# A three-layer graph network with a routed feed-forward block on one core: search rows, step sums, the surplus matmul and the rows' copies change their places

## The chip, the cores and the metric

One Trainium2 chip; the kernel runs on one of its cores. The metric is the device time of one execution in microseconds (us), the median of several runs.

## The reference

6250 nodes with 256 features, 200000 edges sorted by their target.

```python
def _layernorm(x): return (x - mean(x)) / sqrt(var(x) + 1e-5)

src, dst = edges + one loop per node
dinv = rsqrt(segment_sum(1, dst))
def conv(h, W, b): return segment_sum((h @ W)[src] * dinv[src] * dinv[dst], dst) + b

h = layernorm(x)
h = relu(conv(h, W1, b1)); h = relu(conv(h, W2, b2)); x = x + conv(h, W3, b3)

n = layernorm(x)
weights = n @ wr + br                 # one per node
sel = the (6250 // 2 - 1) nodes of highest weight
y = (gelu(n[sel] @ w1 + b1) @ w2 + b2) * weights[sel]
out = x + n + scatter(y, sel)
```

## The kernel before, in words

Nodes are taken in 49 tiles of 128. Each layer multiplies a matrix of edge counts (target by source) with scaled rows of features. For most target tiles (32, 32 and 34 in the three layers) that matrix is built densely as fp16 from one-hots and multiplied tile by tile; a (target tile, source tile) product of 128x128 by 128x512 is a *unit*, run by `unit` (L1403). For the remaining sparse tiles Pool gathers single rows by indirect DMA (`fetch_row`, L2021), and a step with a one-hot sums them (L1412). 5749 units stand in one written-out order `UNIT`; everything else is hung on unit numbers: `SUM_AT`, `SPILL_AT`, `OVER_AT`, `TURN_AT`, `ROWS_TURN_AT` and so on. Each engine runs its instructions strictly in its own written order. TensorE follows `units(limit)`, DVE and ACT follow `upto(limit)` over the same numbers, SP walks them at the end of its queue.

**Front.** The edges must be found first: the kernel counts, for 10 columns of windows, how many edges lie below each window. DVE and ACT count over a coarse list, Pool fetches one search row for each window (L1926), and DVE's `lows` counts in those rows (L846) and makes `step_cols` ("low of step zero", L851). TensorE's `chunk_steps` (the step sums, L1581, 56 instructions) spreads them to the steps, DVE's `place_steps` (L857 to L859) turns them into edge addresses, first for 6 chunks and then for 13, and Pool's `fetch_edges` (L1932) brings the edges. Beside this, the first product of each of the 49 tiles (x times the centred W1) is made by `product_first` (L1361) and copied out by ACT (`out_first`, L1722). Of those, `BEFORE` stand ahead of the step sums, `BESIDE` right behind them, two for each step j in the loop over the batches of edges, and `LATE` near its end. ACT and DVE also measure x's variance: `measure_x(n)` (L866 to L871) takes the seven tiles of one group, and its end lets SP fetch another group (`fetch_x`, L2084). TensorE's 190 ns loads at L1602 belong to a small product in the same stretch. In the batch loop DVE unpacks edges, TensorE transposes them and ACT copies them out.

**Building and layer one.** From unit 98 on, dense tiles are built from pairs of steps (`step`, L1375: one-hots from DVE, evacuated by ACT, L1756) while units of layer one run in between, at the pace of `DUE`.

**Surplus.** A window can hold more edges than its quota; the rest goes through a loop of at least one round (`spill`, in Pool, TensorE and ACT). Pool fetches a list entry, edges, the old sums and, once SP has stored the layer's rows (`rows_out`), the rows themselves (L1995), and makes a one-hot (L1997 to L2001). TensorE multiplies (L1444) when its unit counter reaches `SPILL_AT[l]`, ACT copies (L1797), Pool adds and stores (L2008 to L2011) and raises `overflowed`. SP then fetches the stored sums for each target tile (L2158, from unit `OVER_AT`), ACT scales them (L1766), and DVE's `sum_tile` (L1050, L1052) adds them to the tile's PSUM bank. The unit that starts a tile in a bank waits for the sum of the bank's previous tile.

**Choice and feed-forward.** When the early tiles of layer three are done, a first list of nodes is chosen and their rows are gathered. The first block has four groups of 128 rows. `turn` (L1484) transposes a group on TensorE into one PSUM bank at units 5721, 5727, 5733 and 5739, and waits for DVE's copy of the group before it; `settle` (L1206) is that copy. DVE reaches all four copies at unit 5743, behind the norms (L1103 to L1120) of the tiles summed just before. The hidden layer (L1497) begins behind the last unit.

Of the kernel before, what the change touches and what calls it, by code (L numbers as in the profile page):

```python
# [20 lines left out]
TILES = -(-N // P)  # L21
# [154 lines left out]
GROUPS = TILES // KC  # L176
# [47 lines left out]
UNITS = len(UNIT)  # L224
START = [min(u for u, (p, i) in enumerate(UNIT) if p == q) for q in range(len(Q))]
END = [max(u for u, (p, i) in enumerate(UNIT) if p == q) + 1 for q in range(len(Q))]
SPILL_AT = [2 * TILES + 32, START[TILES] + 85, START[2 * TILES] + 85]
OVER_AT = [SPILL_AT[0] + 2, SPILL_AT[1] + 50, SPILL_AT[2] + 50]


def sum_units():
# [27 lines left out]
BLOCKS = blocks_of()  # L259
# [5 lines left out]
TIES_AT = COUNT_AT[-1] + COUNT_SPACE  # L265
LISTING_AT = TIES_AT + 55
ROWS_TURN_AT = [UNITS - 28 + 6 * s for s in range(len(BLOCKS[0]))]
ROWS_SETTLE_AT = UNITS - 6
NORM_AT = [SUM_AT[2 * TILES + NORM_FROM[g + 1] - 1] if g != EARLY_GROUPS else
           max(SUM_AT[2 * TILES + NORM_FROM[g + 1] - 1], LISTING_AT + 3) for g in range(len(NORMS))]  # L270
TURN_AT = [u + 12 for u in SUM_AT]
# [52 lines left out]


DUE = due_units()
BEFORE, BESIDE, LATE = 10, 3, 6
DVE_COLS = 4
ACT_GROUPS, DVE_GROUPS = (0, 2, 4, 6), (1, 3, 5)
STAGE = (0, 1, 2, 1, 0, 1, 2)  # L330
# [185 lines left out]
def graph(nc, ctx, space, gathered_in, ones, route, small, smalli, b1_sb, br_b, x, x_turned, dst_rows, dst_over, dst_last, edges, gw, gb, wr, br, w1, b1, w2, b2, pair_dram, out):  # L516
# [269 lines left out]
    with nc.Block() as block:  # L786
        @block.vector
        def _(dve):
# [6 lines left out]
            def done(ins, name=None):  # L795
                noted(ins, name)
                dve.wait_ge(c_dve, steps["all"])
# [63 lines left out]
            def measure_x(n):  # L861
                g = DVE_GROUPS[n]
                s, tiles = slice(g * KC, g * KC + KC), staged[STAGE[g]]
                dve.wait_ge(x_in[STAGE[g]], 16 * (STAGE_TURN[g] + 1))
                for i in range(KC):
                    noted(dve.bn_stats(stats[:, i, :], tiles[:, i]))  # L866
                dve.wait_ge(c_dve, steps["all"])
                for i in range(KC):
                    noted(dve.bn_aggr(aggr[:, 0, i, :], stats[:, i, :]))
                dve.wait_ge(c_dve, steps["all"])  # L870
                dve.tensor_copy(spread_of[:, s], aggr[:, 0, 0:KC, 1]).then_inc(measured, 1)  # L871
# [8 lines left out]
            dve.wait_ge(p_order, 1)  # L880
            done(dve.tensor_copy(ordered[:, 1:2], disorder))
            done(dve.tensor_scalar(ordered[:, 0:1], ordered[:, 1:2], 0.0, None, ALU.is_equal))
            measure_x(0)
            lows()
            dve.wait_ge(c_pool, CONSTANTS + LATER_CONSTANTS)
            noted(dve.tensor_copy(iota_two[:], iota16[:].unsqueeze(2).broadcast_to([P, WC, 2])))
            done(dve.tensor_copy(iota_many[:], iota16[:, 0:P].unsqueeze(2).broadcast_to([P, P, 4])))
            place_steps(0)
            place_steps(1)

# [350 lines left out]
            def upto(limit):  # L1241
                for u in range(at["u"] + 1, limit + 1):
# [18 lines left out]
                        spread(0)  # L1261
                    if u == LISTING_AT + 1:
                        take_list(0)
                    if u == ROWS_SETTLE_AT:
                        for s in BLOCKS[0]:
                            settle(s)
                    for q in LOWS.get(u, ()):
                        low_tile(q)
                    if u == MEASURE_AT:
# [623 lines left out]
        def _(pool):  # L1893
# [55 lines left out]
            def each(ins):  # L1949
                ins.then_inc(more_step, 1)  # L1950
                pool.reg_add(m, m, 1)
                pool.wait_ge(more_step, pool.snap(m))
                pool.sem_inc(passed, 1)
# [10 lines left out]
            def spill(l):  # L1964
# [10 lines left out]
                with pool.Fori(0, again):  # L1975
                    each(pool.memset(which, 0.0))
                    with pool.Fori(0, inner):
# [12 lines left out]
                        pool.indirect_dma_start(more_old[:, 0:width], None, target,  # L1990
                                                bass.IndirectOffsetOnAxis(target_i, 0)).then_inc(old_in, 16)
                        landed(more_in)
                        if l >= 0:
                            pool.wait_ge(rows_out[l], 16 * (TILES if l else GROUPS))
                            pool.indirect_dma_start(more_rows, None, row_dram[l],  # L1995
                                                    bass.IndirectOffsetOnAxis(pair_i[:, 1:2], 0)).then_inc(more_rows_in, 16)
                        each(pool.tensor_copy(node, pair_i[:, 0:1]))  # L1997
                        each(pool.tensor_tensor(node, node, item[:, 1:2], ALU.subtract))
                        each(pool.tensor_scalar(bad, node, wide, 16384.0, ALU.is_ge, ALU.mult))
                        each(pool.tensor_tensor(node, node, bad, ALU.add))  # L2000
                        each(pool.tensor_scalar(more_hot, iota16[:, 0:P], node, None, ALU.is_equal))  # L2001
                        if l >= 0:
                            landed(more_rows_in)
                        pool.sem_inc(more_ready, 1)
# [244 lines left out]
```

## Time and profile before

| | before |
|---|---|
| median of 3 runs | 1876.97 us (1875.36 to 1879.09) |
| profiled execution | 1876.37 us |
| its span, first to last instruction | 1874.6 us |
| TensorE (PE) busy | 1808.8 us, 96% |
| VectorE (DVE) busy | 1072.4 us, 57% |
| ScalarE (ACT) busy | 509.8 us, 27% |
| GpSimd (POOL) busy | 1107.0 us, 59% |
| mean granted clock of TensorE | 0.982 |

A line of the timeline gives start and length in us, engine, source line, operation, output<-input, how many instructions are merged, and in brackets how long the engine was idle before and what released it. PEld is TensorE's loading of weights, which overlaps its matmuls. The granted clock is 1.00 at 2.4 GHz and 0.50 at 1.2 GHz. A matmul's end is modelled, so neighbours overlap in the listing.

### The profile page before, as it was taken

How to read it: one execution, taken by the hardware profiler on the slowest of the kernel's cores; microseconds unless marked ns; L12 is line 12 of the kernel's file. 1: busy time of each engine (PE TensorE's matmuls, PEld its weight loads, DVE VectorE, ACT ScalarE, POOL GpSimd, SP SyncE). 2: the span in 40 equal slices, each digit the busy share in tenths (PEclk: the TensorE clock that was granted, in tenths of full speed). 3: DMA queues.
4: the chain of work that ended last, by engine and by line, in shares of the span. 5: the costliest groups of instructions: out<-in, count | busy, mean ns of one | idle time of the engine just before them, and what ended most of it. 6: DMA issues, size and time to landing. Idle time of an engine off the chain costs nothing.

```text
span 1874.6 us, 28149 instructions
## 1 busy us (share of the span) xinstructions
PE 1808.8 (96%) x10093; PEld 1060.7 (57%) x10093; DVE 1072.4 (57%) x2904; ACT 509.8 (27%) x1043; POOL 1107.0 (59%) x1198
## 2 busy tenths in 40 slices
PE   7998999999999999999999999999999999989898
PEld 6765666666665555555555555544444444447655
DVE  6898999888876666432222222216455656866422
ACT  6755423444444445121111111110000000012020
POOL 6423666665656664277777777727777777731401
PEclk8979999999999999999999999999999999999999
DMA  9626566576655665677777777757987888660200
GB/s 322 217 85 246 181 211 214 203 250 232 214 199 177 206 212 179 242 243 240 248 245 241 236 235 235 231 183 274 330 312 271 313 283 303 226 211 36 87 15 21
DMA packets 170640, 403.36 MB, mean 215 GB/s; under 512 B 29612, under 2 KB 122722, under 8 KB 157833
## 3 DMA queue, kind: packets, MB, share of 16 engines
q1 hardware_dynamic: 119856, 263.42, 39.4%
q0 software_dynamic: 50592, 138.13, 23.3%
q8 instruction: 84, 1.38, 0.3%
q14 instruction: 52, 0.42, 0.1%
q10 hardware_dynamic: 56, 0.03, 0.0%
HBM read 282.57 MB, written 118.89 MB: 214 GB/s over the span
## 4 chain that ended last, share of the span: by engine, by line
PE 83%; DVE 8%; DMA 5%; ACT 2%; issue 1%; POOL 1%; POOLq 0%; DVEq 0%; ACTq 0%
PE ag L1403 28%; PE pw L1403 22%; PE ag L1412 10%; PE pw L1375 7%; PE pw L1497 3%; DMA space_rows<-extra,space_rows 3%; PE both L1429 2%; PE pw L1429 2%; PE ag L1510 2%; PE pw L1510 2%; PE ag L1497 1%; PE both L1421 1%; ACT space_ring L1756 1%; DMA space_rows<-deg_dram,space_rows 1%; DVE space_tables L1011 1%
## 5 line engine op out<-in xcount | busy, mean ns | idle before, releaser
L2021 POOL DMA_INDIRECT space_rows<-row_dram,src_s x947 | 965.8, 1020 | 396.1 <-issue 201.1
L1403 PE MATMUL ag<-space_a,space_ring 128*128 128x512 f16 x2107 | 621.6, 379 | 6.3 <-DVE space_work L1052 5.8
L1412 PE MATMUL ag<-space_rows,hots 128*128 128x512 f16 x947 | 359.1, 379 | 5.8 <-DVE space_b L1052 5.8
L1375 PE MATMUL pw<-space_tables 128*128 128x147 f16 (+1 forms) x2022 | 323.0, 243 | 13.5 <-ACT space_ring L1756 10.1
L1375 PEld LDWEIGHTS pw<-space_tables 128*128 128x128 f16 x2022 | 226.6, 114 | 189.5 <-ACT space_ring L1756 22.0
L1756 ACT ACTIVATE space_ring<-pw 128x784 f16<-128x784 f32 (+1 forms) x257 | 219.1, 857 | 231.6 <-PE pw L1375 224.6
L1011 DVE TENSOR_TENSOR space_tables<-iota_two,space_tables 128x588 f16<-128x588 f16 (+1 forms) x506 | 256.2, 506 | 0.0
L1403 PEld LDWEIGHTS ag<-space_a,space_ring 128*128 128x128 f16 x2107 | 197.0, 97 | 98.3 <-DVE space_work L1052 6.0
L1007 DVE TENSOR_TENSOR space_tables<-iota_many,space_tables 128x512 f16<-128x512 f16 x506 | 211.8, 419 | 17.9 <-PE pw L1375 16.6
L1403 PE MATMUL pw<-space_b,space_ring 128*128 128x512 f16 x735 | 189.3, 379 | 0.0
L1403 PE MATMUL pw<-space_a,space_ring 128*128 128x512 f16 x686 | 168.6, 381 | 0.0
L1766 ACT ACTIVATE space_work<-space_work,per_node 128x256 f32<-128x256 f32 x147 | 73.7, 503 | 334.0 <-DMA space_work<-extra 334.0
L1412 PEld LDWEIGHTS ag<-space_rows,hots 128*128 128x128 f16 x947 | 107.2, 113 | 81.2 <-DVE space_b L1052 7.5
L1057 DVE SCALAR_TENSOR_TENSOR space_a<-pw,per_node,space_a 128x256 f16<-128x256 f32 x49 | 23.7, 484 | 207.3 <-ACT space_a L1780 207.3
L1774 ACT ACTIVATE space_work<-both,gb_sb 128x128 f32<-128x128 f32 x196 | 61.2, 364 | 247.3 <-PE both L1421 247.3
L1403 PEld LDWEIGHTS pw<-space_b,space_ring 128*128 128x128 f16 x735 | 71.9, 98 | 78.5
L1403 PE MATMUL ag<-space_b,space_ring 128*128 128x512 f16 x441 | 115.1, 379 | 0.0
L1403 PEld LDWEIGHTS pw<-space_a,space_ring 128*128 128x128 f16 x686 | 67.5, 99 | 79.0 <-issue 1.9
L1064 DVE TENSOR_TENSOR hots<-iota_many,key_s 128x512 f16<-128x512 f16 x238 | 106.5, 460 | 1.2
L1050 DVE SCALAR_TENSOR_TENSOR space_work<-ag,per_node,space_work 128x256 f32<-128x256 f32 x78 | 37.6, 482 | 80.8 <-PE ag L1403 56.1
L1403 PE MATMUL pw<-space_a,space_tables 128*128 128x512 f16 x294 | 78.0, 389 | 0.0
L1050 DVE SCALAR_TENSOR_TENSOR space_b<-pw,per_node,space_work 128x256 f32<-128x256 f32 x20 | 9.7, 483 | 111.0 <-PE pw L1403 77.8
(424 smaller groups left out, 1925.5 us busy)
## 6 DMA issues: line engine op xcount, KB each, us to landing
space_ring<-adj SPq DMA_DIRECT2D x48, 1568.0 KB, 7.4
adj<-space_ring SPq DMA_DIRECT2D x34, 1568.0 KB, 6.1
space_tables<-adj SPq DMA_DIRECT2D x17, 1568.0 KB, 7.3
space_work<-extra SPq DMA_DIRECT2D x147, 128.0 KB
space_rows<-row_dram,src_s POOLq DMA_INDIRECT x947, 4.0
extra<-space_tables SPq DMA_DIRECT2D x14, 896.0 KB
space_b<-in_x_turned SPq DMA_DIRECT2D x7, 896.0 KB, 14.9
space_a<-in_x SPq DMA_DIRECT2D x7, 896.0 KB, 9.4
```

The lines of the kernel that those rows point to most:

```text
L1007: dve.tensor_tensor(olo[:, r], iota_many[:], slo[:, 2 * j:2 * j + 4].unsqueeze(1).broadcast_to([P, P, 4]), ALU.is_equal)
L1011: dve.tensor_tensor(ohi[:, r, :, 0:n], iota_two[:, 0:n].unsqueeze(1).broadcast_to([P, 2, n, 2]), keys.unsqueeze(2).broadcast_to([P, 2, n, ...
L1064: dve.tensor_tensor(hots_area[:, n % (HOTS // 4)], iota_many[:], key_s[:, s:s + 4].unsqueeze(1).broadcast_to([P, P, 4]), ALU.is_equal).the ...
L1375: pe.matmul(pw[v % 2][:, half, at_c:at_c + n], olo[:, j % RING // 2, :, j % 2 * 2 + i], ohi[:, j % RING // 2, j % 2, 0:n, i], start=s == F ...
L1403: mm = pe.matmul(bank(q), a[:, k, :], hh[l][:, k, :], start=i == 0, stop=i == TILES - 1)
L1412: pe.matmul(bank(q), hots_area[:, hot_at, :, g - SPOT_GROUPS[SPOT_GROUP_OF[g]][0]], slots[g % GR], start=i == 1, stop=i == n).then_inc(g_u ...
L1429: mm = pe.matmul(ph[l - 1], fresh[:, q % 2, f, :], gw_sb[:, l, f, :], start=f == 0, stop=f == HALVES - 1)
L1497: mm = pe.matmul(bank_of(hidden_banks[h % 3])[:, 0:n], w1_sb[:, k, m * P:(m + 1) * P], xt[c][:, k, 0:n], start=k == 0, stop=k == HALVES - 1)
L1510: mm = pe.matmul(bank_of(out_banks[s % 2])[0:n, 0:D], hid[c % 2][:, m, i * P:i * P + n], w2_sb[:, m, :], start=m == 0, stop=m == HM - 1)
L1756: act.activation(target[:, :, d:d + n].rearrange("p s (h d) -> p s h d", h=2), pw[v % 2][:, :, 0:n // 2 * TILES].rearrange("p h (d s) -> p ...
L1766: act.activation(ep[:, q % 2], ep[:, q % 2], ACT.Copy, scale=unfactor[:, l, t:t + 1]).then_inc(e_scaled, 1)
L2021: pool.indirect_dma_start(slots[g % GR], None, row_dram[STEP_LAYER[g]], bass.IndirectOffsetOnAxis(src_s[:, s:s + 1], 0)).then_inc(g_in[g % ...
```

## The change

Five edits. (1) The surplus matmul of layer one goes from unit 130 to unit 116; the unit from which sums are fetched, 132, stays. (2) `BEFORE` is 12 in place of 10, so two first products go ahead of the step sums, and the loop beside the batches has two fewer (it ends one step sooner). (3) DVE's first `measure_x` stands behind `lows` and two copies of iotas, ahead of `place_steps`. (4) Each of the first block's four copies stands one unit behind its turn (5722, 5728, 5734, 5740). (5) In Pool's `spill`, the rows' fetch with its wait stands behind the five small instructions that make the one-hot.

```diff
-SPILL_AT = [2 * TILES + 32, START[TILES] + 85, START[2 * TILES] + 85]
-OVER_AT = [SPILL_AT[0] + 2, SPILL_AT[1] + 50, SPILL_AT[2] + 50]
+SPILL_AT = [2 * TILES + 18, START[TILES] + 85, START[2 * TILES] + 85]
+OVER_AT = [SPILL_AT[0] + 16, SPILL_AT[1] + 50, SPILL_AT[2] + 50]
...
-ROWS_SETTLE_AT = UNITS - 6
+ROWS_SETTLE_AT = {u + 1: s for s, u in enumerate(ROWS_TURN_AT)}
...
-BEFORE, BESIDE, LATE = 10, 3, 6
+BEFORE, BESIDE, LATE = 12, 3, 6
...
             done(dve.tensor_scalar(ordered[:, 0:1], ordered[:, 1:2], 0.0, None, ALU.is_equal))
-            measure_x(0)
             lows()
             dve.wait_ge(c_pool, CONSTANTS + LATER_CONSTANTS)
             noted(dve.tensor_copy(iota_two[:], iota16[:].unsqueeze(2).broadcast_to([P, WC, 2])))
             done(dve.tensor_copy(iota_many[:], iota16[:, 0:P].unsqueeze(2).broadcast_to([P, P, 4])))
+            measure_x(0)
             place_steps(0)
             place_steps(1)
...
-                    if u == ROWS_SETTLE_AT:
-                        for s in BLOCKS[0]:
-                            settle(s)
+                    if u in ROWS_SETTLE_AT:
+                        settle(ROWS_SETTLE_AT[u])
...
                         landed(more_in)
-                        if l >= 0:
-                            pool.wait_ge(rows_out[l], 16 * (TILES if l else GROUPS))
-                            pool.indirect_dma_start(more_rows, None, row_dram[l],
-                                                    bass.IndirectOffsetOnAxis(pair_i[:, 1:2], 0)).then_inc(more_rows_in, 16)
                         each(pool.tensor_copy(node, pair_i[:, 0:1]))
                         each(pool.tensor_tensor(node, node, item[:, 1:2], ALU.subtract))
                         each(pool.tensor_scalar(bad, node, wide, 16384.0, ALU.is_ge, ALU.mult))
                         each(pool.tensor_tensor(node, node, bad, ALU.add))
                         each(pool.tensor_scalar(more_hot, iota16[:, 0:P], node, None, ALU.is_equal))
+                        if l >= 0:
+                            pool.wait_ge(rows_out[l], 16 * (TILES if l else GROUPS))
+                            pool.indirect_dma_start(more_rows, None, row_dram[l],
+                                                    bass.IndirectOffsetOnAxis(pair_i[:, 1:2], 0)).then_inc(more_rows_in, 16)
                         if l >= 0:
                             landed(more_rows_in)
```

## Rows read from the trace of the kernel before

**Rows 1.** The page: the chain that ended last, by engine.
```profile
PE 83%; DVE 8%; DMA 5%; ACT 2%; issue 1%; POOL 1%; POOLq 0%; DVEq 0%; ACTq 0%
```

**Rows 2.** TensorE's waits, whole span: us in total, times, longest.
```profile
PE pw L1484 <- DVE space_b L1206: 10.1, 3, 6.2
...
PE ag L1403 <- DVE space_work L1052: 5.8, 1, 5.8
PE ag L1581 <- DVE step_cols L851: 4.8, 1, 4.8
```

**Rows 3.** Timeline of the front, 23 to 48 us.
```profile
23.40 1.38 POOL L1926 DMA_INDIRECT space_rows<-in_dst_rows,tile_i  x1 [0.30 <-DVE space_ring L838]
...
28.36 2.39 DVE L866 BATCH_NORM_STATS2 stats<-space_a 128x6 f32<-128x256 f32 x7
...
29.16 1.03 PE L1361 MATMUL ag<-gw_sb,space_b 128*128 128x256 f32 x4
...
31.47 0.34 DVE L846 TENSOR_SCALAR_CACHE_REDUCE space_rows<-space_rows,cols 128x128 f32<-128x128 f32 x1
...
34.95 12.11 PE L1581 MATMUL ag<-step_cols,space_ring 128*128 128x3 f32 x56 [4.77 <-DVE step_cols L851]
...
36.02 0.99 SPq L2084 DMA_DIRECT2D space_a<-in_x  x2
...
47.17 0.17 DVE L857 TENSOR_TENSOR step_f<-ag,step_at 128x13 f32<-128x13 f32 x1 [8.09 <-PE ag L1581]
```

**Rows 4.** DMA issues at 23.3 to 23.6 us: count, us to landing.
```profile
space_rows<-in_dst_rows,tile_i POOLq DMA_INDIRECT x1, 6.8
```

**Rows 5.** Stretches: us, PE, PEld, DVE, ACT, POOL busy, PEclk, DMA share, GB/s.
```profile
33.00:34.00 1.00, 0.00 (x0) 0.00 (x0) 1.00 (x9) 0.97 (x5) 0.00 (x0) 0.94 1.08 312
...
35.00:47.00 12.00, 12.00 (x57) 12.00 (x57) 1.04 (x5) 5.23 (x22) 5.76 (x6) 0.50 0.79 226
...
173.00:174.00 1.00, 0.00 (x0) 0.00 (x0) 0.00 (x0) 0.00 (x0) 0.10 (x1) 0.91 0.00 0
...
177.00:180.00 3.00, 2.81 (x11) 1.47 (x12) 2.45 (x8) 0.00 (x0) 2.39 (x3) 0.50 0.97 363
...
1665.00:1666.00 1.00, 0.00 (x0) 0.00 (x0) 0.96 (x5) 0.00 (x0) 0.00 (x0) 0.73 0.82 269
```

**Rows 6.** Weight loads of two lines: ns min/median/max, first and last start.
```profile
L1581 PEld LDWEIGHTS ag<-step_cols,space_ring x56: 286/333/333, 35.0 to 46.6; 128*128 128x128 f32 x56
...
L1602 PEld LDWEIGHTS ag<-cols,space_rows x2: 190/191/192, 51.7 to 51.8; 128*128 128x128 f32 x2
```

**Rows 7.** Timeline, the last two products beside the batches.
```profile
89.24 1.03 PE L1361 MATMUL ag<-gw_sb,space_b 128*128 128x256 f32 x4
...
90.10 1.03 PE L1361 MATMUL both<-gw_sb,space_b 128*128 128x256 f32 x4
```

**Rows 8.** Timeline of Pool: the surplus rows of layer one.
```profile
154.45 0.94 POOL L1995 DMA_INDIRECT space_rows<-row_dram,space_rows  x1 [34.41 <-DMA row_dram<-space_a]
...
157.77 1.13 POOL L2001 TENSOR_SCALAR space_rows<-iota,space_rows 128x128 f16<-128x128 f16 x1 [0.21 <-POOL space_rows L2000]
```

**Rows 9.** Timeline of TensorE around the surplus matmul of layer one.
```profile
160.57 0.59 PE L1403 MATMUL ag<-space_a,space_ring 128*128 128x512 f16 x2
...
165.18 0.38 PE L1444 MATMUL both<-space_rows 128*128 128x512 f16 x1
...
177.19 1.03 PE L1403 MATMUL ag<-space_a,space_ring 128*128 128x512 f16 x2 [5.79 <-DVE space_work L1052]
```

**Rows 10.** Timeline around the first block's turns and copies.
```profile
1661.76 0.17 DVE L1103 TENSOR_SCALAR rstd_x<-aggr 128x3 f32<-128x3 f32 x1
...
1665.88 0.42 DVE L1206 COPY space_b<-pw 128x256 f32<-128x256 f32 x1
...
1666.44 0.66 PE L1484 MATMUL pw<-ident,space_b 128*128 128x128 f32 x2 [6.22 <-DVE space_b L1206]
...
1672.59 2.32 PE L1403 MATMUL pw<-space_a,space_tables 128*128 128x512 f16 x10
```

## The prediction, made before the changed kernel was run

> **What bounds the kernel now.** I read the page's chain first, then TensorE's waits, then the timeline around the places the diff touches. TensorE holds 83% of the chain that ended last [rows 1]. So what counts is where it stands still or runs at half its clock, and any such time that goes away before its long middle is carried to the end: the list of TensorE's waits has nothing longer than 1 us behind which Pool's row fetches or a DMA stand. Of its five longest entries three lie where the diff works [rows 2]: 4.8 us for the step sums (L1581) behind DVE's `step_cols`, 5.8 us in layer one behind DVE's first tile sum (L1052), and 10.1 us in three waits of the rows' turns (L1484) behind DVE's copies (L1206), 6.2 of it in one. 0.2% of this kernel, about 3.8 us, is what a measurement can tell from no change.
>
> **Search rows and two products (front).** Before, DVE measures seven tiles of x from 28.36 us and only then counts the search rows from 31.47, so 3.1 us stand ahead of the count; TensorE's tenth product starts at 29.16 and ends at 30.19, the step sums start at 34.95 [rows 3]. Nothing in the rows needs that order. The last search row is issued at 23.40 and takes 6.8 us to land, 30.2 [rows 3, 4]; the ten counts start at 28.4 and want the last row 9 steps of 0.27 later, about 30.8, which leaves 0.6 us. So `step_cols` is ready at about 31.8. TensorE now has two more products in its gap; at 0.86 us from start to start, as at 89.24 and 90.10 [rows 7], they end at 29.16 + 1.72 + 1.03 = 31.9. The sums start at 31.9, **3.0 us** sooner. The measuring itself lands in DVE's wait for the sums, which was 8.09 us long before its end at 47.17 [rows 3]: from about 32.5 (behind the two iota copies) to 35.7. It signals SP's fetch of x group 3, which SP's own queue let go only at 36.02 [rows 3], so that costs nothing; without that cover it would cost up to the 3.2 us of the measuring. ACT's two extra copies go between its squares, and it is idle later; nothing.
>
> **The clock of the step sums.** TensorE has no work between 30.19 and 34.95; in it the granted clock falls (0.94 in 33 to 34) and the sums run at 0.50, the 1.2 GHz level, all of 35 to 47 [rows 3, 5]. With the products up to 31.9 the sums begin at 2.4 GHz. A sum is a weight load with three columns behind it, and the load took 333 ns at half clock where the same form took 190 ns at full (L1602) [rows 6]; the second of the two L1602 loads started 0.11 us behind the first, against 12.11/56 = 0.216 a sum at half clock [rows 3]. So I take two sums for one as long as the full level lasts. How long it lasts no row shows for such work: after TensorE fell idle the level was lost some 3.7 us later here (0.94 is 0.12 us at half), 2.4 us later at 171.4, 5.2 us later at 1660.2 [rows 5, 9, 10]. I take 3.7, the nearest, which saves as much: **3.7 us**, from 0 to 6 (all 56 at full clock).
>
> A load of the weights does not get faster with the clock by the Trainium skill, "TensorE: Matmul & The Clock Gate", section "LDWEIGHTS (loading the stationary operand)": it prices a load by its columns at a fixed rate, with no warm and cold form beside it. By that the 3.7 would be 0 and the change worth that much less. The trace disagrees: 190 against 333 ns.
>
> The two products are missing later in the loop beside the batches: the pair at 89.24 and 90.10 goes [rows 7], 1.7 us of TensorE in a stretch where DVE's unpacking and TensorE's transposes wait for each other in turn, and no row shows which of them would be last without it. I take something under half: **0.7 us**, 0 to 1.7. From 47 to 131 us the front is DVE's and TensorE's own work in turn, so all of this moves the start of layer one. Pool's edge fetches (19 at 1.25 us) start at 36.2 in place of 39.3 and feed batches well ahead.
>
> **Surplus matmul 14 units sooner.** In layer one TensorE passes the matmul (L1444) at 165.18 without waiting for it; from there Pool's add and store, SP's fetch, ACT's scaling and DVE's two sums run in one chain until TensorE goes on at 177.19, 12.0 us later, after 5.79 us of standing still [rows 9]. In units and pairs the 116th unit ends ahead of 160.57 [rows 9]; put there, the chain ends at 172.6, TensorE arrives at 171.4 as before, and 1.2 us of stall are left: **4.6 us**. ACT's spill copy keeps its place right behind an evacuation. What must be there by 160.6: Pool fetched the surplus rows at 154.45, when layer one's rows were stored, and its one-hot was done at 158.90 [rows 8]; the new order of Pool's copies takes the one-hot into the wait of 34.41 us, so that only the landing is left. That part I cost at nothing, since TensorE's margin, 6.3 us before, is still 1.6. In layers two and three the same order only fills Pool's waits; TensorE does not wait there. The stall also cost the clock: it fell in 173 to 174, and 177 to 180 ran at 0.50 [rows 5], so 3 us of work went at half speed. A stall of 1.2 should not lose it: **1.5 us** more, 0 to 2. Next late is that 1.2.
>
> **Rows' copies behind their turns.** TensorE's second turn waits 6.22 us for DVE's first copy, which stands behind three tiles' norms: DVE takes `rstd_x` at 1661.76 and copies at 1665.88 [rows 10]. In the new order the first copy follows that instruction at once: 1661.93 to 1662.35, and with the 0.14 between the old copy's end and TensorE's start, the turn goes at 1662.5 in place of 1666.44. The copies take 0.42 each between norms of about 1.2; the turns then come every 1.55 us or so (six units at 0.216 and a turn), which DVE meets within 0.3 us. Six, six and ten units and three turns later the last unit ends at about 1668.4; before, it ended at 1672.59 + 2.32 = 1674.9 [rows 10], with 1665 to 1666 already at 0.73 of the clock [rows 5]. **6.5 us**, down to 4.7 if the 2.3 us that are left still cost the clock. The norms' end moves from 1665.9 to 1667.3, ahead of the next tile sum. Everything behind it (chosen rows, hidden layer) hangs on the last unit or on this sum.
>
> **Sum.** 3.0 + 3.7 + 0.7 + 4.6 + 1.5 + 6.5 = 20.0 us. The profiled execution took 1876.37 us around its span of 1874.6; that is 0.6 below the median of the runs, 1876.97. So 1856.4 for a profiled one and 1857 for the median. By the bounds: least 2.5 (the last search row half a us late) + 0 + 0 + 3.2 (1.4 lost to ACT in the new chain) + 0 + 4.7 = 10.4, most 3.1 + 6 + 1.7 + 4.7 + 2 + 6.6 = 24.1.
>
> **Rivals.**
> Rival one: the sums run no faster (a load bound by something other than the clock, or the level falls at once). For it: f32 loads were never seen in a long row at full clock. Against: 190 and 333 ns [rows 6]. It takes 3.7 off: 1860.7. The skill's rule above is this rival.
> Rival two: the shortened stalls still lose the clock. For it: the stall at 171.4 lost it after 2.4 us, and 2.3 us are left at the turns. It takes 1.5 + 1.8 off: 1860.3.
> Rival three, slower: the surplus matmul itself becomes the wait. It stands in TensorE's order, so from 160.6 on each us by which Pool's rows are late is a us of TensorE, with the pairs and evacuations behind it. It outweighs the rest only from 20 us of lateness on, a landing behind 180 us. For it: the Pool fetch sits behind 34 us of row stores. Against: the one-hot, already behind that wait, was done at 158.9 [rows 8].
> Rival four: the parts move and the end does not, because something beside TensorE paces the middle (Pool's 947 row fetches). Against: none of TensorE's listed waits [rows 2] is for them. Under 3.8 us gained.
>
> **How the numbers follow.** Forecast 0.70 (its own range 1854 to 1860), rival one 0.12, rival two 0.12, rival four 0.04, rival three 0.02. Rivals one and two are faster too, so faster is 0.94. The range takes in the forecast and both of them together (1864) and reaches 1865 for a late chain at the surplus; low, 1853, is every bound at its best.
>
> **What would show it.** Right: L1581 starting at about 32 with no wait before it, and a clock of 1.00 in its first microseconds; DVE's second `step_f` at about 40 to 41; L1444 some 4.6 us nearer to layer one's first unit, and the wait of L1403 behind L1052 near 1 us; the first L1206 ahead of the last norms, and the turns' wait near 2.3 us. Wrong: L1444 with a wait for Pool, a new wait of L846 for a DMA, or the later layers longer by what the front gave.

## The result, and the profile after

The changed kernel takes 1859.37 us (median of 6 executions, 1858.35 to 1862.86) against 1877.24 us before (median of 6): a ratio of 0.9908, interval 0.9898 to 0.9919. By the medians that is 17.9 us, 0.95%, faster; 20.0 us were forecast, and 1859.4 lies in the range of 1853 to 1865. The profiled execution took 1858.35 us around a span of 1856.6, 18.0 us less than before. Behind line 1264 a line of the kernel after has a number one lower than before (L1403 is L1402, L1444 is L1443, L1484 is L1483, L1581 is L1580); only among the moved lines, in DVE's front and in Pool's `spill`, is the offset another.

From the page after, busy time by engine, and the chain by engine:

```profile
PE 1801.6 (97%) x10093; PEld 1056.3 (57%) x10093; DVE 1071.9 (58%) x2904; ACT 510.1 (27%) x1043; POOL 1098.4 (59%) x1198
...
PE 80%; DVE 8%; DMA 7%; ACT 2%; issue 1%; POOL 1%; POOLq 0%; DVEq 0%; ACTq 0%
```

TensorE does the same 10093 matmuls in 7 us less busy time, and its page has 11 us less idle time around them; it is still the chain. TensorE's waits after, whole span (us in total, times, longest), against [rows 2]:

```profile
PE pw L1483 <- DVE space_b L1206: 6.1, 3, 2.8
...
PE ag L1402 <- DVE space_work L1052: 1.4, 1, 1.4
```

The wait of the step sums is gone from the list, that for the first tile sum fell from 5.8 to 1.4, and the longest of the rows' turns from 6.2 to 2.8 us (one of the second block now; the first block's is 2.28). The front after, against [rows 3]:

```profile
28.38 0.35 DVE L846 TENSOR_SCALAR_CACHE_REDUCE space_rows<-space_rows,cols 128x128 f32<-128x128 f32 x1
...
31.64 0.17 DVE L851 SCALAR_TENSOR_TENSOR step_cols<-cols 128x10 f32<-128x10 f32 x1
...
32.01 9.52 PE L1580 MATMUL ag<-step_cols,space_ring 128*128 128x3 f32 x56
...
35.70 0.15 DVE L857 TENSOR_TENSOR step_f<-ag,step_at 128x6 f32<-128x6 f32 x1
...
41.63 0.17 DVE L857 TENSOR_TENSOR step_f<-ag,step_at 128x13 f32<-128x13 f32 x1 [5.51 <-PE ag L1580]
```

The counts of the search rows start 3.1 us sooner and wait for no row; the sums start behind the twelfth product with no wait, and take 9.52 us in place of 12.11. The granted clock (the column ahead of DMA share and GB/s) in stretches of the kernel after, against [rows 5]:

```profile
34.00:35.00 1.00, 1.00 (x10) 1.00 (x9) 0.97 (x3) 0.97 (x5) 0.00 (x0) 0.83 1.21 294
35.00:44.00 9.00, 9.00 (x37) 8.55 (x38) 3.04 (x22) 6.63 (x29) 5.84 (x7) 0.50 0.87 236
...
166.00:170.00 4.00, 3.29 (x27) 2.24 (x28) 3.96 (x12) 0.00 (x0) 3.09 (x4) 1.00 0.95 375
...
1648.00:1650.00 2.00, 0.00 (x0) 0.00 (x0) 1.83 (x7) 0.43 (x2) 0.00 (x0) 1.00 0.80 266
1650.00:1656.00 6.00, 5.86 (x29) 3.08 (x30) 4.51 (x17) 0.17 (x1) 0.00 (x0) 1.00 0.66 219
```

The sums run at 2.4 GHz until 34.66 (0.83 is two thirds of a microsecond at full) and then at 1.2. TensorE's record has no gap there, so the clock fell while the sums ran, and not behind a wait. Behind the shortened stall of the surplus (TensorE goes on at 166.71), and in and behind the turns' wait, the clock stays full. Surplus and turns after, against [rows 8 to 10]:

```profile
115.45 0.64 POOL L1996 TENSOR_SCALAR space_rows<-iota,space_rows 128x128 f16<-128x128 f16 x1 [0.21 <-POOL space_rows L1995]
...
148.27 1.07 POOL L1999 DMA_INDIRECT space_rows<-row_dram,space_rows  x1 [32.18 <-DMA row_dram<-space_a]
...
154.27 0.38 PE L1443 MATMUL both<-space_rows 128*128 128x512 f16 x1
...
166.71 0.60 PE L1402 MATMUL ag<-space_a,space_ring 128*128 128x512 f16 x2 [1.43 <-DVE space_work L1052]
...
1649.37 0.17 DVE L1103 TENSOR_SCALAR rstd_x<-aggr 128x3 f32<-128x3 f32 x1
...
1649.57 0.42 DVE L1206 COPY space_b<-pw 128x256 f32<-128x256 f32 x1
...
1650.14 0.41 PE L1483 MATMUL pw<-ident,space_b 128*128 128x128 f32 x2 [2.28 <-DVE space_b L1206]
...
1653.57 2.32 PE L1402 MATMUL pw<-space_a,space_tables 128*128 128x512 f16 x10
```

The one-hot starts 33 us ahead of the rows' fetch, the matmul does not wait, the stall is 1.43 us, and the first copy follows `rstd_x` at once. Where the 18.0 us came from, by the start of the same instruction in both traces:

| place | before | after | gained so far |
|---|---|---|---|
| second `step_f` | 47.17 | 41.63 | 5.54 |
| first unit of layer one | 131.09 | 124.88 | 6.21 |
| TensorE goes on behind the first tile sum | 177.19 | 166.71 | 10.48 |
| transposes of that tile's result (L1421) | 182.31 | 170.18 | 12.13 |
| first gathered step (L1412) | 200.05 | 189.13 | 10.92 |
| surplus matmul of layer three | 1248.48 | 1237.96 | 10.52 |
| first turn | 1658.55 | 1646.18 | 12.37 |
| hidden layer | 1674.74 | 1655.73 | 19.01 |
| end of the span | 1874.6 | 1856.6 | 18.0 |

Three steps have no edit near them: 1.2 us lost between 182 and 200, 1.9 won between 1248 and 1658, 1.0 lost behind the hidden layer's start.

### The profile page after: what moved, and what is told of

It reads as the page before. It is cut to its first block, busy times and chain, and to the rows that moved or that the text cites. A ratio compares the mean times of both kernels' runs of the same rounds, so it can differ in the third digit from the quotient of the medians.

```text
span 1856.6 us, 28149 instructions
## 1 busy us (share of the span) xinstructions
PE 1801.6 (97%) x10093; PEld 1056.3 (57%) x10093; DVE 1071.9 (58%) x2904; ACT 510.1 (27%) x1043; POOL 1098.4 (59%) x1198
## 4 chain that ended last, share of the span: by engine, by line
PE 80%; DVE 8%; DMA 7%; ACT 2%; issue 1%; POOL 1%; POOLq 0%; DVEq 0%; ACTq 0%
PE ag L1402 28%; PE pw L1402 21%; PE ag L1411 10%; PE pw L1374 7%; PE pw L1496 3%; DMA space_rows<-extra,space_rows 2%; PE pw L1428 2%; PE both L1428 2%; PE ag L1509 2%; PE pw L1509 2%; PE ag L1496 1%; PE both L1420 1%; ACT space_ring L1755 1%; DMA space_work<-extra 1%; DVE space_tables L1011 1%
## 5 line engine op out<-in xcount | busy, mean ns | idle before, releaser
L1402 PE MATMUL ag<-space_a,space_ring 128*128 128x512 f16 x2107 | 620.3, 378 | 1.9 <-DVE space_work L1052 1.4
L1402 PEld LDWEIGHTS ag<-space_a,space_ring 128*128 128x128 f16 x2107 | 196.7, 97 | 94.0 <-DVE space_work L1052 1.6
L1402 PE MATMUL pw<-space_b,space_ring 128*128 128x512 f16 x735 | 189.3, 379 | 0.0
L1402 PE MATMUL pw<-space_a,space_ring 128*128 128x512 f16 x686 | 167.2, 379 | 0.0
L1402 PEld LDWEIGHTS pw<-space_b,space_ring 128*128 128x128 f16 x735 | 71.8, 98 | 78.5
L1402 PE MATMUL ag<-space_b,space_ring 128*128 128x512 f16 x441 | 115.1, 379 | 0.0
L1402 PEld LDWEIGHTS pw<-space_a,space_ring 128*128 128x128 f16 x686 | 67.3, 99 | 77.8
L1402 PE MATMUL pw<-space_a,space_tables 128*128 128x512 f16 x294 | 75.5, 379 | 0.0
```

The costliest lines, as they stand in the source:

```text
L1402: mm = pe.matmul(bank(q), a[:, k, :], hh[l][:, k, :], start=i == 0, stop=i == TILES - 1)
```

## Experiments

Each is the changed kernel with the edit shown, timed in 4 to 6 executions beside the kernel before (medians there 1876.94 to 1877.23).

**Copies back at one unit.**

```diff
-ROWS_SETTLE_AT = {u + 1: s for s, u in enumerate(ROWS_TURN_AT)}
+ROWS_SETTLE_AT = UNITS - 6
```

> The changed kernel with one edit undone: the four copies of the rows stand at one unit again, behind the norms. Theory (the parts add): the second turn waits 6.2 us again, TensorE falls to 1.2 GHz in it, and the 6.6 us that lay between the first turn and the hidden layer come back: 1859.4 + 6.6 = 1866.0 us. Rival (the hidden layer would have waited for something else, the chosen rows or the list): under 2 us come back, 1859.4 to 1861.4 us.

1865.54 us (ratio 0.9939, 0.9926 to 0.9952), 6.2 more than the changed kernel: the theory holds. TensorE at the second turn and at the hidden layer:

```profile
1656.88 0.66 PE L1484 MATMUL pw<-ident,space_b 128*128 128x128 f32 x2 [6.21 <-DVE space_b L1206]
...
1665.14 1.88 PE L1497 MATMUL ag<-space_b,space_ring 128*128 128x512 f32 x4
```

From the first turn (1649.00) to the hidden layer it is 16.14 us, as before (16.19), against 9.55 in the changed kernel. In the trace the edit is worth its 6.6 us, and the medians, 6.2 apart, agree: nothing behind it takes much of them.

**Surplus matmul back at unit 130.**

```diff
-SPILL_AT = [2 * TILES + 18, START[TILES] + 85, START[2 * TILES] + 85]
-OVER_AT = [SPILL_AT[0] + 16, SPILL_AT[1] + 50, SPILL_AT[2] + 50]
+SPILL_AT = [2 * TILES + 32, START[TILES] + 85, START[2 * TILES] + 85]
+OVER_AT = [SPILL_AT[0] + 2, SPILL_AT[1] + 50, SPILL_AT[2] + 50]
```

> The changed kernel with the surplus matmul back at unit 130. Theory one (the stall alone counts, as its clock was taken back by the fetch of the next tile's stored sums): the wait for the first tile sum is 5.8 us instead of 1.4, and the time is 1859.4 + 4.4 = 1863.8 us. Theory two (the clock counts too, as predicted): 1859.4 + 4.4 + 1.6 = 1865.4 us. They differ in where the first gathered step of layer one starts against that of the changed kernel (189.1 us): 193.5 by theory one, 195.1 by theory two.

1865.41 us (0.9940, 0.9927 to 0.9952), 6.0 more; first gathered step at 195.34. Theory two holds: the clock counts. TensorE goes on at 171.41 after 5.71 us, and the stretches around it are at half clock:

```profile
168.00:171.00 3.00, 0.00 (x0) 0.00 (x0) 0.61 (x2) 1.01 (x2) 2.06 (x3) 0.51 0.84 309
171.00:174.00 3.00, 2.59 (x11) 1.48 (x12) 2.53 (x7) 0.00 (x0) 2.39 (x3) 0.50 0.96 369
```

The 1.2 us that the changed kernel gave back between 182 and 200 have another source than the place of the surplus matmul. In the changed kernel the third tile's stored sums, issued by SP at 173.09, were scaled by ACT at 182.06, 9.0 us later; before it was 185.01 and 192.97, 8.0 us. Here it is 9.0 again (179.23 and 188.27). All twelve traces with twelve products ahead of the sums have 8.6 to 9.2, and the only other one with ten has 7.8. So every kernel with twelve paid it; two traces with ten do not show that the products are the cause, and it stays open.

**x measured first again.**

```diff
+            measure_x(0)
             lows()
...
-            measure_x(0)
             place_steps(0)
```

> The changed kernel with the measuring of x ahead of the search rows' counts again; twelve products still stand ahead of the step sums. Theory (the clock falls in the gap behind the last product): step_cols at about 34.9, TensorE idle 3 us from 32.0, the sums at 1.2 GHz for nearly all of their length, second step_f at 46.8 to 47.2 in place of 41.6, time 1859.4 + 5.3 = 1864.7 us. Rival (two more products carry the clock into the sums, so that only the 3.0 us of the start are lost): second step_f at 44.6, time 1862.4 us.

1865.03 us (0.9940, 0.9928 to 0.9952), 5.7 more. The theory holds, though the second `step_f`, at 46.42, is 0.4 us sooner than it says. TensorE's sums, and DVE's second addresses:

```profile
34.90 11.42 PE L1580 MATMUL ag<-step_cols,space_ring 128*128 128x3 f32 x56 [2.78 <-DVE step_cols L851]
...
46.42 0.17 DVE L857 TENSOR_TENSOR step_f<-ag,step_at 128x13 f32<-128x13 f32 x1 [8.09 <-PE ag L1580]
```

The clock fell at 35.7 (0.84 in 35 to 36), 0.8 us into the sums; two more products ahead do not carry the level over a gap of 2.8 us.

**Ten products again.**

```diff
-BEFORE, BESIDE, LATE = 12, 3, 6
+BEFORE, BESIDE, LATE = 10, 3, 6
```

> The changed kernel with ten products ahead of the step sums again. Theory (the level is lost some 3.7 us behind the last product, whatever sums run in between): the sums start at 31.9 behind an idle 1.7 us, the granted clock falls at about 33.9 instead of 34.7, second step_f at 42.3 in place of 41.6; with the two products back in the loop beside the batches, 0.7, the time is 1859.4 + 1.4 = 1860.8 us. Rival (the sums start at 1.2 GHz at once after the gap): second step_f at 44.2, 1859.4 + 2.6 + 0.7 = 1862.7 us. Second rival (products in the loop hide fully): 1859.4 + 0.7 = 1860.1 us.

1861.15 us (0.9911, 0.9897 to 0.9926), 1.8 more, with 1858.72 to 1865.24 too wide to part 1.4 from 0.7. In its trace the sums start at 31.78 behind 1.45 us of idleness, the clock falls at 34.16, and the second `step_f` is at 41.86, 0.2 later than in the changed kernel: the rival of a cold start is out. So the sums begin at full clock without the two products too, once the search rows are counted first. The profiled execution was the slowest one, 1865.24 us, and most of what it lost lies far from the edit:

```profile
156.65 3.03 POOL L2007 TENSOR_TENSOR space_rows<-space_rows 128x256 f32<-128x256 f32 x1 [5.49 <-DMA space_rows<-extra,space_rows]
```

Pool's add of the surplus took 3.03 us in place of 0.93, a later small instruction 1.93 in place of 0.23, and TensorE's stall behind the tile sum was 4.61 in place of 1.43. In layer three this execution lost 1.6 us more (see the last run).

**Pool's old order.** The rows' fetch and its wait stand ahead of the five small instructions.

```diff
+                        if l >= 0:
+                            pool.wait_ge(rows_out[l], 16 * (TILES if l else GROUPS))
+                            pool.indirect_dma_start(more_rows, None, row_dram[l],
...
                         each(pool.tensor_copy(node, pair_i[:, 0:1]))
...
-                        if l >= 0:
-                            pool.wait_ge(rows_out[l], 16 * (TILES if l else GROUPS))
-                            pool.indirect_dma_start(more_rows, None, row_dram[l],
```

> The changed kernel with Pool's old order in the surplus loop: the fetch of the rows, with its wait, stands ahead of the five small instructions again. Theory (costed at nothing): the fetch is issued at 148.3 us as in the changed kernel, the five instructions end some 4.5 us later (as from 154.45 to 158.90 before), at 152.8, the surplus matmul is reached at 154.3 and does not wait: 1859.4 us, within 0.5. Rival (the five instructions are stretched beside VectorE's one-hots, as Pool's add was in the run with ten products, 3.03 us instead of 0.93): the matmul waits, its stall and that behind it grow by 1 to 3 us, 1860.4 to 1862.4 us.

1858.68 us (0.9911, 0.9897 to 0.9925): no difference, as the theory has it. The one-hot, and with it all that the matmul needs of Pool's own work, ends at 153.07:

```profile
152.36 0.71 POOL L2000 TENSOR_SCALAR space_rows<-iota,space_rows 128x128 f16<-128x128 f16 x1 [0.21 <-POOL space_rows L1999]
```

TensorE passes the matmul at 154.44 without waiting. The edit is a margin of a microsecond, not a gain.

**Surplus at unit 112.**

```diff
-SPILL_AT = [2 * TILES + 18, START[TILES] + 85, START[2 * TILES] + 85]
-OVER_AT = [SPILL_AT[0] + 16, SPILL_AT[1] + 50, SPILL_AT[2] + 50]
+SPILL_AT = [2 * TILES + 14, START[TILES] + 85, START[2 * TILES] + 85]
+OVER_AT = [SPILL_AT[0] + 20, SPILL_AT[1] + 50, SPILL_AT[2] + 50]
```

> The changed kernel with the surplus matmul four units sooner still, unit 112. The rows landed at 152.6 us, the matmul would be reached at about 152.8. Theory: it does not wait or by some tenths, the 1.4 us that are left of the stall behind the first tile sum go, and the time is 1859.4 - 1.3 = 1858.1 us. Rival (the third tile's stored sums, fetched later by SP, set the pace): the stall goes, the next product's wait grows by as much, 1859.4 us.

1861.50 us (0.9915, 0.9901 to 0.9929): no gain, inside the spread. Neither theory holds: TensorE does not wait at the matmul, but the stall is 1.11 us, not 0. TensorE was at the matmul only at 154.48, because its clock came back at 129.5 at the start of layer one, not at 126.8; and from the matmul to the end of the stall it is 13.88 us, against 12.44 in the changed kernel's trace. Pool's small instruction behind the store took 1.98 us in place of 0.23. Pool's instruction and VectorE's next one behind a pause, in the changed kernel and then here:

```profile
161.74 0.23 POOL L2012 TENSOR_SCALAR space_rows<-space_rows 128x1 f32<-128x1 f32 x1 [1.79 <-DMA extra<-space_rows]
161.96 0.23 DVE L1018 TENSOR_TENSOR space_ring<-space_ring,ident 128x128 f16<-128x128 f16 x1 [0.30 <-ACT space_ring L1755]
```

```profile
161.61 1.98 POOL L2012 TENSOR_SCALAR space_rows<-space_rows 128x1 f32<-128x1 f32 x1 [1.78 <-DMA extra<-space_rows]
163.94 0.25 DVE L1018 TENSOR_TENSOR space_ring<-space_ring,ident 128x128 f16<-128x128 f16 x1 [0.43 <-ACT space_ring L1755]
```

In the changed kernel the instruction falls into a pause between VectorE's one-hots. Here it comes into their unbroken row and ends when the row does. The other kernel with the matmul at unit 112 (all edits, below) has the same 1.98, 13.88 and 1.12. So the four units bring the matmul forward and lengthen the chain behind it by about as much.

The front of this execution is the clearest view of the sums; its DVE, its loads (ns min/median/max), and its clock:

```profile
39.03 0.17 DVE L857 TENSOR_TENSOR step_f<-ag,step_at 128x13 f32<-128x13 f32 x1 [2.98 <-PE ag L1580]
...
42.85 0.29 DVE L916 TENSOR_TENSOR space_work<-space_ring,step_base 128x128 f32<-128x128 int32 x1 [3.05 <-DMA space_ring<-in_edges,step_i]
```

```profile
L1580 PEld LDWEIGHTS ag<-step_cols,space_ring x56: 186/192/338, 31.8 to 38.5; 128*128 128x128 f32 x56
```

```profile
32.00:37.00 5.00, 5.00 (x47) 5.00 (x46) 3.91 (x20) 4.93 (x23) 0.75 (x1) 1.00 0.93 234
37.00:38.00 1.00, 1.00 (x8) 1.00 (x8) 0.00 (x0) 0.97 (x4) 0.69 (x2) 0.65 0.56 131
```

With the same code in the front the level held until 37.3. 46 loads in 5 us are one every 0.109 us. The second `step_f` came 2.6 us sooner than in the changed kernel's trace, and all of it went into a wait of 3.05 us for the first edges: DVE's first unpacking (L916) starts at 42.85, there at 42.56.

**Row copies further ahead.**

```diff
-ROWS_SETTLE_AT = {u + 1: s for s, u in enumerate(ROWS_TURN_AT)}
+ROWS_SETTLE_AT = {UNITS - 26: 2, UNITS - 19: 3}
...
+                        if q == len(Q) - 2:
+                            settle(0)
                         sum_tile(q)
+                        if q == len(Q) - 2:
+                            settle(1)
```

> The changed kernel with the first row copy ahead of the tile sum that precedes it on VectorE, the second right behind that sum, the third and fourth ahead of the norms of the late group. Theory: the second turn's wait of 2.28 us goes (VectorE is at that sum at 1646.7 us, the first turn ends at 1646.8), the hidden layer starts up to 2.2 us sooner and the time is 1859.4 - 2.0 = 1857.4 us. Rival (VectorE is the bound there: sums and norms in one row, so the copies only move the wait to the third or fourth turn): under 0.5 us gained.

1858.34 us (0.9904, 0.9890 to 0.9918). First turn to hidden layer is 7.56 us against 9.55, so the theory's 2.0 us are there in the trace; one wait is left, at the fourth turn (L1487 is this kernel's number for L1483):

```profile
1654.25 0.41 PE L1487 MATMUL pw<-ident,space_b 128*128 128x128 f32 x2 [0.45 <-DVE space_b L1206]
```

In the median only 1.0 shows, less than these runs can tell apart.

**Three products between the sums.**

```diff
+            between = {5: BEFORE, 9: BEFORE + 1, 13: BEFORE + 2}
             for c in range(CH):
                 chunk_steps(c)
-            for t in range(BEFORE, BEFORE + BESIDE):
-                product_first(t)
+                if c in between:
+                    product_first(between[c])
```

> The changed kernel with the three products that follow the step sums put between them, behind the 6th, 10th and 14th chunk. Theory one (the granted clock falls because the sums alone do little, and a product between them holds it): clock 1.00 through 32 to 40, second step_f at 40.8 us in place of 41.6, first transposes of the batches at 43.9 in place of 45.8, time 1859.4 - 1.9 = 1857.5 us. Theory two (the level is lost a few us into the sums all the same): the products run at half clock ahead of the last sums, second step_f at 46 to 47, first transposes at about 49, time 1859.4 + 3.2 = 1862.6 us.

1865.07 us (0.9937, 0.9923 to 0.9951), 5.7 more, and neither theory holds. The clock stayed at 1.00 until 38.2, nearly as theory one has it, but the time went theory two's way for a reason in neither:

```profile
41.75 2.05 PE L1360 MATMUL both<-gw_sb,space_b 128*128 128x256 f32 x4 [2.74 <-ACT space_b L1722]
```

The third product needs a bank that ACT copies out only behind its squares; TensorE stood still, and the last 12 sums ran behind it at half clock. Second `step_f` 46.26.

**First addresses ahead of the measuring.**

```diff
-            measure_x(0)
             place_steps(0)
+            measure_x(0)
             place_steps(1)
```

> The changed kernel with the first addresses of steps ahead of the measuring of x. Theory (the run with the surplus at unit 112 had its second step_f at 39.0 us and its first unpacking waited 3.05 us for the first edges, fetched behind the first step_f at 35.6): first step_f at about 34.5, so the first edges land near 41.5; with the second step_f at 41.4 to 41.9, as in most runs, nothing is gained, 1859.4 us; if it comes at 39, the first unpacking waits about 2 us and not 3. Rival (the measuring, now up to 37.8 us, holds up SP's fetch of x, which before came at 36.5, and with it the products): 0.5 to 1.5 us lost.

1860.08 us (0.9908, 0.9895 to 0.9921): no gain, as the theory has it for a second `step_f` at 41.87. The first one came at 35.01 only, 1.95 us behind the start of the sums, and these started only at 33.06, behind products that ran later in this execution. What earlier addresses give when the second `step_f` comes at 39 was not seen.

**The same, and two products between the sums.** Behind the 6th and the 12th chunk, the third product behind the sums.

```diff
+            between = {5: BEFORE, 11: BEFORE + 1}
...
-            for t in range(BEFORE, BEFORE + BESIDE):
+                if c in between:
+                    product_first(between[c])
+            for t in range(BEFORE + 2, BEFORE + BESIDE):
                 product_first(t)
```

> As the kernel with the addresses first, and with two of the three products that follow the step sums put between them (behind the 6th and the 12th chunk); for the third ACT's copies would be late. Theory: clock 1.00 up to at least 38 us, the 56 sums and two products end at 40.2 to 40.6, second step_f at about 40.5, first unpacking at 41.5 by its edges in place of 42.6, time 1859.4 - 1.1 = 1858.3 us. Rival (the third product, at half clock behind the sums, and the transposes take it back): 1859.4 us.

1864.40 us (0.9932, 0.9920 to 0.9945), 5.0 more: theory and rival both missed. The clock fell at 36.9 (0.96 in 36 to 37) although a product had run from 34.90, and the second product stood at half clock ahead of the last 20 sums:

```profile
39.00 2.05 PE L1360 MATMUL ag<-gw_sb,space_b 128*128 128x256 f32 x4
40.84 4.27 PE L1580 MATMUL ag<-step_cols,space_ring 128*128 128x3 f32 x20
```

Second `step_f` 45.15. A product between the sums is a sure 0.9 to 1.8 us on the path against a level that it may or may not hold (until 38.2 in the run before, 36.9 here).

**All of them.** The last edit with the copies further ahead and the surplus at unit 112.

> The changed kernel with the addresses first, two products between the sums, the copies of the rows ahead of the tile sum and its norms, and the surplus matmul at unit 112. Theory (parts add): 1.1 + 1.9 + 0.3 less, 1859.4 - 3.3 = 1856.1 us; the wait for the rows' copies at most 0.5 us. Rival (what the front gives is taken back before the first unit of layer one): 1857.4 us.

1861.32 us (0.9914, 0.9901 to 0.9927): both missed, for the products between (second `step_f` 45.23, clock down at 36.5); turn to hidden layer again 7.56 us. Of the versions tried none beats the changed kernel by more than these runs can tell; the copies further ahead are the one edit with a gain of its own in the trace.

**The changed kernel again,** unaltered.

> The changed kernel itself, unaltered, for the spread between executions. Theory (the clock's falls and rises come at times that differ between executions of the same work): median 1859.4 us, second step_f between 39 and 42 us, full clock at the start of layer one between 125.7 and 129.7 us; single executions from 1858 to 1863 us. Rival (the differences of the other runs come from their edits): step_f at 41.6, clock back at 126.6, as in the first profile.

1858.60 us (0.9897, 0.9883 to 0.9911), 1856.99 to 1862.70. The theory holds, with wider spans than I gave: the second `step_f` at 40.53, the clock down at 35.8 in the sums and back only at 131.3 at the start of layer one, and the fastest execution a microsecond below the span. The profiled execution is the one of 1862.70. Stretches of its clock, and a wait in layer three:

```profile
35.00:36.00 1.00, 1.00 (x10) 1.00 (x10) 0.93 (x11) 1.00 (x7) 0.00 (x0) 0.88 1.02 146
```

```profile
PE ag L1411 <- DVE space_b L1052: 2.6, 1, 2.6
```

```profile
1532.00:1536.00 4.00, 3.92 (x19) 1.85 (x20) 3.76 (x14) 0.51 (x1) 2.64 (x3) 1.00 0.40 114
```

The same wait in the kernel before, and the stretch behind it:

```profile
PE ag L1412 <- DVE space_b L1052: 2.6, 1, 2.6
```

```profile
1539.00:1542.00 3.00, 3.00 (x9) 1.10 (x8) 2.82 (x10) 0.51 (x1) 1.99 (x2) 0.53 0.49 161
```

A wait of 2.6 us cost the clock before and did not here. From the third surplus matmul to the first turn it is 410.07 us before and 408.22 in the first trace of the changed kernel, and every other run has one of the two lengths (408.1 to 408.4, or 409.7 to 410.2), the one with the copies put back 410.2. In all six traces with the longer one the clock fell at this wait, in the eight others it held. So the 1.9 us won there come from the clock's level at one wait that no edit touches, and five of the twelve later runs lost them again. From the hidden layer to the end it is 199.86 before, 200.87 after, and others have either (199.6 to 199.9 in three, 200.7 to 201.0 in nine): the 1.0 us lost there can come with and without these edits, and what decides it stays open.

## Why the prediction held, and where it did not

**Step sums sooner, 3.0.** Right: 34.95 to 32.01 is 2.94, and no row was late. It is not so in each execution: in four traces (Pool's old order, addresses first, and the two kernels built on that) the products ended later and the sums started at 33.05 to 33.21. The prediction puts the measuring at nothing, and that is not quite so: DVE takes the first `step_f` only behind it, at 35.70 and without a wait. With the first addresses ahead it came 1.95 us behind the start of the sums, which would be 33.96 here (an estimate from that run). So the first edges are asked for some 1.7 us later than they could be, and they are the next to be late; what that costs is not shown. Undone with the clock that goes with it, the earlier count costs 5.7 us.

**Full clock in the sums, 3.7.** That the sums run faster at full clock is right, the size was off: 2.6 in this execution (5.54 less 2.94). A load of this form runs at 192 ns and every 0.109 us at full clock, over 46 of them in a row; so rival one falls, and with it, for these f32 loads, the pricing of the Trainium skill, "TensorE: Matmul & The Clock Gate", "LDWEIGHTS (loading the stationary operand)", without a clock. The step that failed is "the level was lost some 3.7 us later here ... I take 3.7, the nearest". That span was read behind an idle TensorE, and here TensorE was never idle. In the seven traces with the changed kernel's front unaltered the level fell 2.2 to 5.5 us into the sums, 2.9 in the middle one; 3.7 lies in that span, above its middle. And where it held longest it gave nothing more, since the first edges were the next to be late (the unpackings that waited for them start at 42.6 to 43.0): "feed batches well ahead" was the second step that failed. In the changed kernel's trace DVE's first unpacking already waits 0.17 us for them. It starts 5.3 us sooner than before (47.83 to 42.56), and 2.9 of that is the earlier start of the sums, so the clock's term could pass on some 2.3 us, and not 6. And the second `step_f`, at 41.63, was not at the 40 to 41 named as a sign.

**Two products, 0.7.** 6.21 less 5.54 is 0.67, but that it meets the forecast is luck: from the second `step_f` to the first unit it is 83.3 to 84.2 us in the runs with twelve products whose edges were less than 1 us late, and with ten it is 83.9 (before) and 84.6. The term is not shown. Nor is it shown that the two products carry the clock into the sums, since with ten these began at full clock too.

**Surplus, 4.6, and its clock, 1.5.** Right: the matmul is 4.7 us nearer to the first unit (34.09 to 29.39), a stall of 1.43 is left in place of the 1.2 forecast, and 4.3 us arrive where TensorE goes on (10.48 less 6.21); the clock's share was 1.65 at the tile's transposes (12.13 less 10.48). Undone, the two cost 6.0 us against the 6.1 summed. What the text lacked is the next late one, the third tile's stored sums: in all twelve traces with twelve products they took 0.9 to 1.5 us back against before, also with the matmul at its old place, and no run shows why. Rival three had no case: the rows, 4.3 us from issue, landed at 152.6, 1.7 ahead of the matmul.

**Turns, 6.5.** Right: 9.55 in place of 16.19 us from turn to hidden layer is 6.64; wait 2.28, with the clock kept. Rival two, that the shortened stalls still lose it, came true in two executions. Of the ten traces in which the first block's second turn waits 2.3 us, eight have 9.55 or 9.56 and two (Pool's old order, surplus at unit 112) 11.0, for the clock; at the turns it cost 1.5 us there, against the 1.8 priced. PE's second turn and the stretch behind it with Pool's old order:

```profile
1651.50 0.66 PE L1483 MATMUL pw<-ident,space_b 128*128 128x128 f32 x2 [2.29 <-DVE space_b L1206]
```

```profile
1652.00:1654.00 2.00, 2.00 (x6) 0.71 (x5) 1.97 (x7) 0.00 (x0) 0.00 (x0) 0.50 0.80 265
```

The two versions with the copies further ahead have only 0.45 us of such a wait, and in both traces the clock held.

**Pool's order, nothing.** Right: 1858.68 without it.

**Sum.** Undone one by one, measuring 5.7, surplus 6.0 and turns 6.2 make 17.9 of the 17.9 measured; the products' own part lies inside the spread of that sum. That it meets to a tenth is luck: against the changed kernel's second median, 1858.60, the three make 20.2 of 18.6. In the trace the forecast parts come to 18.8, and what was not forecast (1.2 and 0.4 lost, 1.9 won, 1.0 lost) nearly cancels. Rival four is out with it: the middle passes on all that the front gives, as far as the first edges.

## What to carry to other kernels

When a stall is removed, follow what the freed engine asks for next, and give its term that as an upper bound; here the clock of the step sums could pass on 2.3 us, not 6, however long it held. Price what a clock level may give from several executions or as a range: in one kernel the same gap can cost it or not. Look at where a small instruction falls in the row of the engine beside it: four units sooner, it took 1.98 us in place of 0.23. And put a consumer's copies between, not behind, the long work of the engine that makes them, as the turns show: same instructions, 6.6 us.

## What the runs showed of the hardware

**One wait, two outcomes.** Identical stretches of code lost the clock in one execution and kept it in another: 2.6 us in layer three with 0.53 or 1.00 behind it, 1.4 to 2.1 us apart. The wait's length did not decide it there: the six that lost the level waited 2.34 to 2.64 us, the eight that kept it 2.38 to 2.62. It was the same with 2.3 us at the turns, 0.50 or 1.00 behind it, 1.5 us apart. At the start of layer one the full level came back between 0.4 us ahead of the first unit and 4.6 us behind it. Such outcomes are of the size of the spread between executions of one kernel (1858.35 to 1862.86).

**Sums that do not hold the level.** In the changed kernel the granted clock fell in the step sums, 56 weight loads with three columns behind each, with TensorE's record full from 32.01 to 41.39: 0.83 in 34 to 35 and 0.50 from then on.

**VectorE's one-hots and Pool.** In the run with ten products Pool's add of 128x256 took 3.03 us while VectorE's one-hots ran at their usual 0.42 and 0.56 us one behind the other for its first 2.4 us; in the changed kernel's first trace the add took 0.93, and two of VectorE's instructions beside it took 1.09 and 0.95. The 128x1 instruction behind the store shows what went with the longer times. In ten of the 14 traces VectorE paused for 0.28 us or more as it started, and it took 0.23 us. In three (ten products, and the two with the matmul at unit 112) it started inside an unbroken row of one-hots, took 1.93 to 1.98 us and ended within 0.1 us of the start of VectorE's next pause. In the last it started 0.2 us behind a pause and took 0.43. The Trainium skill, "SBUF — State Buffer", "Who interferes with whom", has it that a VectorE instruction with two inputs in SBUF and a GpSimd one that reads SBUF contend, and that the order of issue decides which of them is blocked. The durations agree; it was not tried by itself.
